# A cap on the expert weights that are in flight, with separate semaphores for f1 and f2

## The reference, cut to what matters

```
x = x + attn(layernorm(x))                                # stage A of the kernel
logits = einsum('btd,des->btes', grouped(layernorm(x)), controller) + tie
perm   = (logits == max over the 16 tokens of a group)    # one token per expert and group
sel    = einsum('btd,btes->besd', grouped, perm)          # gather
inner  = relu(einsum('besd,esdf->besf', sel, f1) + bias)  # 1024 -> 64
inter  = einsum('besf,esfd->besd', inner, f2)             # 64 -> 1024
out    = einsum('besd,btes->btd', inter, perm)            # scatter
x      = x + out
```

## Time and profile before

| what | us |
|---|---|
| median of three timed runs | 1400.66 |
| the profiled execution's own time | 1394.15 |
| its span, slowest core (core 5) | 1392.3 |
| spans of the 8 cores | 1382.8 to 1392.3 |
| first expert part, core 5 (first layer1 to last layer2) | 1092.8 to 1153.3 |
| second expert part, core 5 | 1280.7 to 1334.1 |

### The profile page before, as it was taken

One profiled execution on the slowest core, in us unless ns is written; L12 is line 12 of the kernel. 1 busy time (PEld: TensorE's weight loads), 2 busy tenths in 40 slices (PEclk: granted clock), 3 DMA queues, 4 the chain that ended last, 5 costly groups with the idle time before them and its releaser, 6 DMA issues. The chain is left out here.

```text
span 1392.3 us, 68142 instructions; the slowest of 8 cores (1382.8 to 1392.3 us)
## 1 busy us (share of the span) xinstructions
PE 1148.8 (83%) x28864; PEld 692.5 (50%) x28864; DVE 980.6 (70%) x1389; ACT 810.8 (58%) x1187; POOL 672.1 (48%) x566
## 2 busy tenths in 40 slices
PE   1578988889899988889899888885677779887798
PEld 0245555555555555555555555553344556544665
DVE  3167777677777777777777777765778587785776
ACT  0155656555565555555565555654249776488775
POOL 4166766776767766777667766675101000011000
PEclk9799999999999999999999999996569799988999
DMA  9912222222222222222222222123134485750947
GB/s 160 149 44 45 43 51 51 52 48 49 47 51 55 45 49 53 47 53 43 52 50 53 50 47 40 30 34 79 23 94 143 134 263 164 217 184 35 312 135 235
DMA packets 75158, 122.09 MB, mean 88 GB/s; under 512 B 13408, under 2 KB 38000, under 8 KB 74864
## 3 DMA queue, kind: packets, MB, share of 16 engines
q1 hardware_dynamic: 48128, 92.30, 21.8%
q0 software_dynamic: 26736, 25.44, 13.6%
HBM read 117.93 MB, written 41.94 MB: 115 GB/s over the span
## 5 line engine op out<-in xcount | busy, mean ns | idle before, releaser
L829 DVE CAST W<-psW 128x1024 bf16<-128x1024 f32 x160 | 195.5, 1222 | 112.6 <-PE psW L630 112.4
L415 ACT CAST B<-psXY 128x1024 bf16<-128x1024 f32 x128 | 129.9, 1015 | 74.0 <-PE psXY L597 74.0
L1095 POOL TENSOR_TENSOR psel<-permT_sb,gmask_sb 128x256 bf16<-128x256 bf16 x32 | 20.1, 628 | 260.8 <-DVE permT_sb L1327 235.9
L411 ACT CAST A<-psXY 128x1024 bf16<-128x1024 f32 x128 | 129.8, 1014 | 21.2 <-PE psXY L597 21.0
L517 PE MATMUL psD<-wv_sb,xnf 128*128 128x512 bf16 x512 | 128.8, 386 | 13.6 <-DMA wv_sb<-wvT 13.6
L540 PE MATMUL psD<-wq_sb,xnf 128*128 128x512 bf16 x512 | 128.6, 385 | 11.8 <-DMA wq_sb<-wqT 6.4
L508 PE MATMUL psD<-wk_sb,xnf 128*128 128x512 bf16 x512 | 123.6, 386 | 14.6 <-DMA wk_sb<-wkT 11.8
L825 DVE TENSOR_TENSOR AI<-A,eye 128x1024 bf16<-128x1024 bf16 x160 | 131.1, 834 | 1.8 <-ACT A L411 1.3
L569 PE MATMUL psD<-wo_sb,o_fm 128*128 128x512 bf16 x512 | 131.3, 391 | 0.7 <-issue 0.6
L376 POOL TENSOR_TENSOR kt<-kraw,rk 128x1024 bf16<-128x1024 f32 x32 | 60.8, 1902 | 134.4 <-ACT rk L461 134.4
L1108 ACT CAST R<-P 128x1024 bf16<-128x1024 f32 (+1 forms) x128 | 110.1, 905 | 8.3 <-PE P L1187 6.2
(11 more groups left out here) (138 smaller groups left out, 2578.7 us busy)
## 6 DMA issues: line engine op xcount, KB each, us to landing
ring<-f1d SPq DMA_DIRECT2D x64, 256.0 KB, 4.0
ring<-f2d SPq DMA_DIRECT2D x64, 256.0 KB, 5.0
out<-ring SPq DMA_DIRECT2D x64, 256.0 KB, 3.4
xy<-x SPq DMA_DIRECT2D x68, 128.0 KB, 2.4
f1d<-f1w POOLq DMA_DIRECT2D x128, 64.0 KB, 2.6
f2d<-f2w POOLq DMA_DIRECT2D x128, 64.0 KB, 2.7
x1d<-x1b SPq DMA_DIRECT2D x64, 128.0 KB, 2.4
xy<-x1d SPq DMA_DIRECT2D x32, 256.0 KB, 3.5
```

The source lines that it names most:

```text
L411: s.copy(A[k][:], psX).then_inc(s_a, 1)
L415: s.copy(B[k][:], psX).then_inc(s_b, 1)
L829: v.tensor_copy((Wf if k == 5 else W[k % 2])[:], psW[:, 0:1024]).then_inc(s_w, 1)
```

## The change

Among the pairs that reuse a slot (p >= 10), the load of f1 of pair m also waits until f2 of pair m - 2 has landed, and the load of f2 of pair m waits until f1 of pair m - 1 has landed. In the order f1(m), f2(m), f1(m+1), f2(m+1) each transfer so waits for the third before it. For that f2 gets semaphores of its own (`s_v`), a slot's count goes by 16, and layer1 waits for both. The loads of the first ten pairs and the four loads of tiles among the weights get no new wait.

```diff
     s_w = [sem(f"b_w{r}") for r in range(NR)]
+    s_v = [sem(f"b_v{r}") for r in range(NR)]
...
             p = m % 32
-            return 32 * (m // 32 * ((31 - p % NR) // NR + 1) + p // NR + 1)
+            return 16 * (m // 32 * ((31 - p % NR) // NR + 1) + p // NR + 1)
...
                 p = m % 32
                 if p >= NR:
                     y.wait_ge(s_pf2, 2 * (m - NR + 1))
+
+                    y.wait_ge(s_v[(p - 2) % NR], landed(m - 2))
                 y.dma_start(out=w1(p), in_=f1_d[p * 128:p * 128 + 128, :]).then_inc(s_w[p % NR], 16)
-                y.dma_start(out=w2(p), in_=f2_d[p * 128:p * 128 + 128, :]).then_inc(s_w[p % NR], 16)
+                if p >= NR:
+                    y.wait_ge(s_w[(p - 1) % NR], landed(m - 1))
+                y.dma_start(out=w2(p), in_=f2_d[p * 128:p * 128 + 128, :]).then_inc(s_v[p % NR], 16)
...
             def layer1(m):
                 t.wait_ge(s_w[m % 32 % NR], landed(m))
+                t.wait_ge(s_v[m % 32 % NR], landed(m))
```

## The result

The changed kernel takes 1412.59 us (median of 4 runs, 1409.42 to 1415.63) against 1400.56 us for the kernel before (median of 4 runs, the three of the forecast among them). The ratio is 1.0086, with a 95% interval of 1.0065 to 1.0108. Forecast were 1405.1 us and a range of 1391.5 to 1418.5: the sign and the mechanism hold, the size came out almost three times as large, 12.0 us instead of 4.4. Some executions of either kernel show a lower granted clock on the cores of a die and take longer (1441.7 us at 0.82, for one); times and ratios here leave them out.

What follows compares the result with a forecast made beforehand. TensorE, its stops and some slow clock bound the expert parts; under the cap DMA would fix their ends: +5.1 and -0.7 us, +4.4 on 1400.66, giving 1405.1 us (range 1391.5 to 1418.5).

Steps and rivals of the forecast that it cites:

- No cost of the waits and semaphores themselves: Some 88 added waits on SP and 64 on TensorE's sequencer count as 0; at worst 1 us per half.
- The cap binds and TensorE becomes idle for weights from pair 16 to 19 on: Expert parts: 2.3 us per pair for DMA against TensorE's 1.25, so layer1 waits about 1 us each.
- The end of a part is set by the last landing plus 3.0 us: Expert parts: after the last pair lands, TensorE still needs 3.0 us for the remaining layer1, layer2 and ReLU.
- The round: Expert parts: issue of a transfer to issue of the third after it, 3.45 us; three transfers go per round.
- L: Latency of a weight transfer with three in flight, taken as 3.35 us from the gather and scatter parts.
- c: Duration of a round, L plus about 0.1 us to the next issue: 3.45 us; no change in total at 3.30.
- The two parts: First expert part -0.7 us (end 1152.6 against 1153.3), second +5.1 us (1339.2 against 1334.1).
- The parts between: Gather and scatter parts: no cost from moved tile loads; a change over 1 us would show the prediction wrong.
- The stops: TensorE's idle times within groups, 7.6 and 7.0 us per expert part, read as instruction fetches held up behind weights.
- The rule of the Trainium skill that was weighed: DMA engines go round-robin between queues by packet, so the cap would shorten no stop; nothing changes in the forecast sum.
- The faster rival: Expert parts: stops go and DMA keeps up, c 2.8 us, together -15.2 us, 1385.5 us; chance of c < 3.21: 0.22.
- The figure weighed for the faster rival: Skill's 2.0 us + bytes / 436 GB/s gives 2.6 us for 256 KB, putting c at 2.7.

Runs made afterwards that it cites:

- The run with the cap in one part: Cap of three in the second expert part only, none in the first, against the kernel before: ratio 1.0063 (1.0047 to 1.0080).
- the cap of five: In both expert parts each refill waits for the fifth transfer before it instead of the third; against the kernel before: ratio 0.9968 (0.9953 to 0.9983).
- these runs: Refills halved to 128 KB under the change's cap, ratio 0.9970; the changed kernel, 256 KB, 1.0086; one 512 KB transfer per pair, at most two in flight, 1.0100.

## Why the prediction was right in sign and short in size

- **No cost of the waits and semaphores themselves.** Right: ratio 1.0004 with all semaphores and no cap.
- **The cap binds and TensorE becomes idle for weights from pair 16 to 19 on.** Right: the first wait for weights comes at pair 15 to 17 in the first part and 15 to 20 in the second, over the eight cores, and about 13 us a part of them follow. Behind the new waits nothing else came late: between the parts no engine waits for a load of a tile on any core.
- **The end of a part is set by the last landing plus 3.0 us.** Right: 3.1 and 3.2 us in the mean of the cores. On core 2 the last one lands at 1152.1 and the part ends at 1155.1, then 1346.9 and 1350.4.
- **The round.** This is the term that was mis-sized. I put L at 3.35 us and c at 3.45. Measured in the mean are latencies of 3.7 and 3.5 us, and last issues 54.1 and 52.1 us after the first. By the prediction's own formula (14c + 0.7, and in the first part 1.5 for the loads of tiles) that makes c 3.71 and 3.67. The last refill lands 57.8 and 55.2 us after the first is issued, where the prediction has 53.9 and 52.4; that is 6.7 us. The stretches behind L were read as means, and that is what misled. In the gather part the transfers go in threes, xy, f1, f2, and the earlier trace rows has 2.9, 3.4 and 3.6 us for them: the latency grows with the number under way when a transfer is issued. In the mean of the cores it is 2.9 us there with none, 3.1 with one and 3.5 with two. Under a cap of three most refills have two, and 3.5 us is what the second part shows; the first, with its loads of tiles, has 3.7. The shared semaphore, which I had suspected, is not the reason: in that gather stretch f1 and f2 take 3.4 and 3.7 us before, and 3.5 and 3.7 with semaphores of their own. Why the scatter's 3.5 us at 3.1 in flight was low is open; most of its transfers are stores, which share semaphores in pairs.
- **The two parts.** Forecast -0.7 and +5.1 us for core 5; in the mean of the cores the first went from 59.7 to 63.9 (+4.2) and the second from 53.8 to 61.5 (+7.7). The run with the cap in one part puts 8.8 of 12.0 us into the second.
- **The parts between.** I had said that gather and scatter would not change by more than 1 us, and counted more than that as a sign of being wrong. From the end of the first expert part to the start of the second it is 1.2 us more, and 1.0 us more after the second. The 1.0 us are the clock handed over, as shown above core by core. The 1.2 go with the clock too: its mean in this stretch fell from 0.912 to 0.895, and TensorE's busy time rose by 1.6 us. That was a cost left out: a TensorE that waited in short turns hands over a lower clock.
- **Sum.** The expert parts grew by 11.9 us: the 4.4 forecast, 6.7 for the round, and 0.8 for ends 0.1 and 0.2 us longer and for reading core 5 instead of the mean. With the 2.2 us behind the parts it is 14.1. The mean spans of the two profiled executions differ by 15.0; the other 0.9 us stand ahead of the first expert part, where nothing was changed. The medians of the timed runs differ by 12.0, so these two executions overstate the loss by some 2 us.
- **The other signs.** Refills were to be issued 1.15 us apart, over some 50 us, and are 1.26 and 1.21 us apart, over 54.1 and 52.1 us. The first part was to be about as long, and is 4.2 us longer.
- **The stops.** The reading that they are instruction fetches gets support from a thing that the prediction did not look at: in the kernel before, the stops of over 0.3 us stand at the same places on all eight cores, in the first part after 156, 271, 386, 501 or 733 of its 1024 matmuls, 115 or twice 116 apart. With the semaphores of the change, one more wait a pair in TensorE's list, nearly all of them stand after 266, 381, 494 or 608. So their places hang on the list of instructions. How long they are hangs on the weights' traffic: they fall with the cap of three and with the bytes, and without refills they are gone, as far as that profile can be used. The rule of the Trainium skill that was weighed (DMA: Bandwidth & Descriptors, Queues, rings and completion order), by which a fetch waits for one packet at most, would leave the stops as they are; the trace does not agree: in the first 16 pairs they are 4.5 to 7.0 us without a cap and 1.3 with three. Whether the fetch's packet waits on its engine or its latency grows elsewhere isn't told by the trace, and stays open.
- **The faster rival** needed c under 3.21 and got 3.69. Its mechanism was not idle, though: the cap of five is that rival in a milder form, with hardly any waits for weights and a third less stops in the first part.
- **The figure weighed for the faster rival.** In the window of three the mean landing of 256 KB took 3.6 us, and core 2's shortest refill 2.6. The Trainium skill (DMA: Bandwidth & Descriptors, Anatomy of one DMA) has 2.0 us + bytes / 436 GB/s for one transfer issued by GpSimd, by which 128, 256 and 512 KB would take 2.3, 2.6 and 3.2 us (estimates). The means of these runs with others in flight do not agree: 3.0, 3.6 and 4.7 us.

## What to carry to other kernels

A cap on transfers in flight sets a rate, cap / latency; compare it with what the consumer needs in the time that its buffers leave, and read the latency at that depth: of the transfer that has as many ahead of it as the cap will leave, not a mean over a burst, and from one whose semaphore no other one shares. Two costs move against each other here, waits for data when the queue is too shallow and stops that look like stalled instruction fetches when it is too deep, so a sweep of the depth over its whole range (3 to 6, and none) was worth more than any single setting. Averages of latency are not enough near the edge, since one late engine can hold a whole window, as the next section has it.

## What the runs showed of the hardware that was not expected

A window of three can be held up by a single DMA engine. On core 2 three refills issued at 1302.0, 1302.7 and 1303.6 land only at 1307.6, 1308.3 and 1308.9. For 2.25 us before that the queue's packets are these (queue, packets, MB, share of 16 engines):

```profile
DMA packets 35, 0.05 MB, mean 24 GB/s; under 512 B 9, under 2 KB 9, under 8 KB 35
...
q1 hardware_dynamic: 35, 0.05, 7.7%
```

7.7% of sixteen is 1.2 engines, and from 1306.6 on the packets follow one another singly: it seems that one engine works through its share of three transfers while fifteen have nothing to do. TensorE then shows its longest wait, 3.3 us. That the fifteen would have gone on with later transfers without a cap is likely and not tested. An instruction packet of 16 KB, of 0.96 us, stands 1 us ahead of it, at 1305.4 on the same core; that it causes the lag is not shown. Landings of over 5 us come in two such groups of three in this part, in all 6 of its 44; on the other cores there are 0 to 2 of 44 in the second part. So this is a cost of single events, the largest on the slowest core.

A transfer of 64 rows is dear to issue on SP, whatever its size. At least 0.44 us go for 64 rows of 2 KB and 0.47 for the stores' 64 rows of 4 KB (256 KB), against 0.32 for 128 rows of 2 or 4 KB and 0.31 for 32 rows of 4 KB (128 KB). Right behind another transfer it is 0.1 us more. No run shows why.
